# Causal masks, maxima and new turn orders in a four-layer decoder kernel

## The chip, the cores and the metric

The kernel runs on one core of a Trainium2 chip. The metric is the device time of one execution in microseconds (us). Three timed runs of the kernel before gave 1022.54, 1021.28 and 1025.13 us; the median is 1022.54 us.

## The reference

Input is `x` of 8 samples x 128 tokens x 128 features and a context of the same size, all fp32. Four layers follow one another, each an attention over the own tokens ("a"), an attention over the context ("x") and a feed-forward part ("f"), each with a residual and a normalisation. What matters here are the softmax attentions with scores of 128 queries by 128 keys per head:

- L0x: 16 heads of width 8, over the context and over the own tokens. The own tokens are masked causally.
- L1x: 16 heads of width 64, over the context, without a mask.
- L2x: 16 heads of width 8, without a mask.
- L3a: 16 heads of width 64 over the own tokens, masked causally.
- L3x: 8 heads of width 16 with exponential gates, masked causally, whose "D" term is made by the same kind of matrix products.

The others (L0a, L1a, L2a) are linear attentions; L0f, L1f, L2f are mixtures of experts of 9, 8 and 9 feed-forward blocks whose experts are all computed for all tokens.

## The kernel before, in words

The eight samples are taken in pairs (256 tokens). Two streams, a and b, run side by side: a computes pairs 0 and 2, b pairs 1 and 3. Every engine (PE = TensorE, DVE = VectorE, ACT = ScalarE, POOL = GpSimd, SP = the engine that issues DMAs) has one program per stream, written as a generator: each `yield` ends a step. `TURN_ORDER` (L144) is a table of text, one entry per engine, such as "a1 b1 a2 b1": so many steps of a, then so many of b. `take_turns` (L402) follows it, so the order of every engine's instructions is fixed when the kernel is built. Each engine then works strictly in that order, and waits on semaphores where an operand isn't there. Stream a is ahead of b by somewhat less than three stages, so that a softmax attention of one stream mostly lies beside a feed-forward part of the other. Each stream has four banks of PSUM in a ring; a bank is opened again when DVE or ACT has read it.

An attention step for one sample goes like this. `scores8` (L481, heads of width 8) or `scores64` (L771, heads of width 64) makes the scores, queries on the partitions, four heads in each of four banks. DVE takes each row's maximum (`maxima` L1179, `block_maxima` L1187) into `m_wide`, a tile whose columns 32i to 32i+3 hold the four heads of bank i. `turn_maxima` (L473) turns that tile over on PE (L479), and DVE copies the result to `mT` (L1202). Then the scores are made again with the keys on the partitions (`scores8_t` L503, `scores_t` of L1x L793 and of L3a L978), and into the same banks `less_maximum` (L491) adds a matrix product that subtracts the maximum: a column of the constant `pick` (minus one in row j), spread over 128 columns, as weights of 32 rows, and 32 rows of `mT` as the moving operand. ACT takes the exponential of each bank (L1743).

A causal mask is one more product into the same bank: the weights are `ident_bf` (128x128, bf16), and the moving operand is the 128x128 mask in bf16, repeated for the four heads (512 columns). L486, L510, L776, L984 and L1045 are these products. The products of the scores are fp32; each fp32 product is issued as two instructions, each with its own weight load, while a bf16 product is one. So 16 calls of `less_maximum` show as 32 matmuls:

```
def less_maximum(u, i, b, j, last):
    return mm(b[:, j * T:j * T + T], const("pick")[rows32(i), j:j + 1].to_broadcast([32, P]), s.mT[rows32(i), u],
              start=False, stop=last)
```

Products whose weights lie in 32 rows (`rows32`) or 64 rows (`rows64`) use a quarter or a half of the array's rows, and four or two of them can run at once. In L1x's `scores_t` four fp32 scores of 64 rows alternate, head by head, with four `less_maximum` of 32 rows.

At the start, SP loads weights in a fixed order; DVE waits for the constants (`con`), casts three of them to bf16 (L1671) and then begins its turns; ACT waits for the constants too (L2018) before its first table load. `use` (L1680) loads an ACT table when the function that is asked for is not in the table loaded last.

Of the kernel before, what the change touches and what calls it, by code (L numbers as in the profile page):

```python
# [24 lines left out]
ALU = mybir.AluOpType  # L25
# [23 lines left out]
for _n, _w in [("ident", 128), ("neg_causal", 128), ("neg_causal_t", 128), ("causal_t", 128), ("block8", 128),  # L49
               ("ones", 128), ("spread", 128), ("tiny16", 128), ("feats", 64), ("head8in32", 4), ("head16in64", 4),  # L50
               ("pick", 8), ("cos", 8), ("sin", 8), ("eps", 5)]:
    CONST[_n] = (_at, _w)
    _at += _w
# [3 lines left out]
def shape_constants():  # L57
# [9 lines left out]
    put("neg_causal", np.where(p[None, :] > p[:, None], NEG, 0).astype(np.float32))  # L67
    put("neg_causal_t", np.where(p[:, None] > p[None, :], NEG, 0).astype(np.float32))
# [7 lines left out]
    put("head16in64", (p[:, None] % 64 // 16 == np.arange(4)).astype(np.float32))  # L76
    put("pick", -(p[:, None] % 32 == np.arange(8)).astype(np.float32))
# [55 lines left out]
def group_words(g):  # L133
# [23 lines left out]
    "dve":  # L157
# [10 lines left out]
    "act":  # L168
# [8 lines left out]
    "pool":  # L177
        "a1 b1 a1 b2 a3 b1 a1 b1 a1 b1 a3 b1 a1 b2 a1 b2 a1 b1 a4 b1 a2 b4 a1 b2 a2 b2 a1 b1 a3 b1 a1 b2 a1 b2 a1 "
# [2241 lines left out]
```

## Time and profile before

| | |
|---|---|
| timed runs, median (lowest to highest) | 1022.54 us (1021.28 to 1025.13) |
| span of the profiled execution, first to last instruction | 1020.0 us |
| PE matmul busy | 904.2 us, 89% |
| DVE busy | 539.7 us, 53% |
| ACT busy | 450.7 us, 44% |
| POOL busy | 50.8 us, 5% |
| mean share of the full TensorE clock that was granted | 0.952 |
| DMA, mean over the span | 35 GB/s |

The profiled execution has no time of its own besides its span; the span is 2.5 us below the median of the runs, which is what lies around the first and the last instruction. "Busy" of PE is the time in which at least one matmul was in the array, from the modelled start of each to its end. The chain of work that ended last is followed back for only about 1% of the span (the last feed-forward part), so it says nothing of the layers before.

### The profile page before, as it was taken

Reading aid. Unit: us, or ns where it says so; the run is one execution under the profiler, and the core shown is the slowest. Engines: PE = TensorE matmul, PEld = TensorE weight load, DVE = VectorE, ACT = ScalarE, POOL = GpSimd, SP = SyncE. Lnnn points to the kernel's source line nnn. Section 1 sums busy time; section 2 is a strip of 40 time slices with the busy share of each in tenths; the row PEclk is TensorE's granted clock in tenths of the full one; section 3 lists DMA queues with packets and bytes.
Section 4 is the critical chain, followed back from the end, with each engine's and each line's share of the span. In section 5 each row is a group of like instructions: output and inputs, shape, how many; then the busy total and the mean of one; then the engine's idle time right before and its main releaser. Section 6 shows DMA issues by size and latency. Waiting matters only on the chain. (4 is left out here: it accounts for less than half of the span.)

```text
span 1020.0 us, 22561 instructions
## 1 busy us (share of the span) xinstructions
PE 904.2 (89%) x9368; PEld 700.2 (69%) x9368; DVE 539.7 (53%) x1569; ACT 450.7 (44%) x923; POOL 50.8 (5%) x71
## 2 busy tenths in 40 slices
PE   7689899999989998997987979989998989899772
PEld 5257768778778785666556757867887868686441
DVE  5733565653265575347636853655325547454345
ACT  2044343453454673574255233244465446433442
POOL 2300000010010000001000000001001000000000
PEclk8799989999999998999999999999999999999965
DMA  9100000401000301103000000040000030000000
GB/s 344 40 2 3 1 1 1 166 2 37 2 19 1 141 3 40 43 12 139 2 12 1 2 1 2 2 166 33 6 1 19 1 140 1 2 1 2 2 1 21
DMA packets 6838, 36.12 MB, mean 35 GB/s; under 512 B 721, under 2 KB 4305, under 8 KB 5458
## 3 DMA queue, kind: packets, MB, share of 16 engines
q1 hardware_dynamic: 6738, 34.68, 9.1%
q8 instruction: 76, 1.25, 0.5%
q14 instruction: 24, 0.20, 0.1%
HBM read 34.15 MB, written 0.52 MB: 34 GB/s over the span
## 5 line engine op out<-in xcount | busy, mean ns | idle before, releaser
L673 PE MATMUL bank<-xT,weights_F 128*128 128x256 f32 x832 | 202.9, 386 | 3.1 <-ACT p L1818 2.6
L673 PEld LDWEIGHTS bank<-xT,weights_F 128*128 128x128 f32 x832 | 152.0, 193 | 26.8 <-issue 4.2
L681 PEld LDWEIGHTS bank<-weights_F,p 128*128 128x128 f32 x1088 | 133.4, 191 | 18.8 <-DVE p L1363 7.2
L681 PE MATMUL bank<-weights_F,p 128*128 128x128 f32 x1088 | 141.3, 278 | 3.7 <-DVE p L1363 3.0
L1743 ACT ACTIVATE p<-bank 128x512 f32<-128x512 f32 x160 | 84.5, 601 | 121.0 <-PE bank L492 120.9
L1683 ACT ACT_TABLE_LOAD x76 | 97.5, 1283 | 12.9 <-DMA weights_con<-in_con 5.9
L1347 DVE SCALAR_TENSOR_TENSOR res<-bank,comb,res 128x128 f32<-128x128 f32 x184 | 55.7, 345 | 74.1 <-PE bank L681 71.6
L1184 DVE TENSOR_REDUCE m_wide<-bank 128x4 f32<-128x512 f32 x96 | 60.3, 684 | 43.4 <-PE bank L780 33.5
L1818 ACT ACTIVATE p<-bank 128x512 f32<-128x512 f32 x72 | 42.5, 597 | 91.6 <-PE bank L673 91.2
L1363 DVE TENSOR_TENSOR p<-p,bank 128x512 f32<-128x512 f32 x72 | 49.3, 685 | 47.5 <-PE bank L673 27.3
L1894 ACT ACTIVATE p<-bank 128x512 f32<-128x512 f32 x64 | 36.6, 598 | 51.3 <-PE bank L673 51.2
L492 PEld LDWEIGHTS bank<-mT,weights_con 32*128 32x128 f32 x1280 | 46.4, 194 | 17.4 <-issue 13.5
L492 PE MATMUL bank<-mT,weights_con 32*128 32x128 f32 x1280 | 55.1, 296 | 0.0
L1715 ACT ACTIVATE lnv<-mv,weights_con 128x2 f32<-128x2 f32 x56 | 16.6, 296 | 74.7 <-DVE mv L1139 72.7
L1192 DVE TENSOR_REDUCE mx<-bank 128x4 f32<-128x512 f32 x64 | 40.2, 682 | 16.5 <-PE bank L488 16.4
L2037 POOL TENSOR_TENSOR xb<-x_tok,biases 128x256 f32<-128x256 f32 x24 | 19.3, 806 | 575.1 <-DVE x_tok L1147 561.5
L525 PE MATMUL bank<-p,vz 128*32 128x128 f32 x1280 | 42.7, 280 | 4.5 <-ACT p L1743 4.4
L525 PEld LDWEIGHTS bank<-p,vz 128*32 128x32 f32 x1280 | 35.2, 112 | 11.0 <-issue 8.4
L525 PE MATMUL bank<-p,weights_con 128*32 128x128 f32 x1280 | 41.7, 275 | 0.0
L1207 DVE TENSOR_TENSOR attnT<-bank,res 128x128 f32<-128x128 f32 x32 | 9.3, 289 | 55.7 <-ACT res L1748 55.7
L525 PEld LDWEIGHTS bank<-p,weights_con 128*32 128x32 f32 x1280 | 35.9, 111 | 1.0
L1147 DVE TENSOR_SCALAR x_tok<-res,mv,rstd 128x128 f32<-128x128 f32 x88 | 26.4, 343 | 18.1 <-ACT rstd L1716 17.6
(319 smaller groups left out, 1356.0 us busy)
## 6 DMA issues: line engine op xcount, KB each, us to landing
weights_F<-in_L1f SPq DMA_DIRECT2D x2, 4096.0 KB, 13.8
weights_F<-in_L0f SPq DMA_DIRECT2D x2, 3456.0 KB, 13.4
weights_F<-in_L2f SPq DMA_DIRECT2D x2, 3456.0 KB, 12.1
weights_Y<-in_L1x_kv SPq DMA_DIRECT2D x2, 1024.0 KB, 10.6
weights_Z<-in_L1x SPq DMA_DIRECT2D x2, 1024.0 KB, 12.9
weights_Y<-in_L2a SPq DMA_DIRECT2D x2, 898.0 KB, 4.4
weights_Z<-in_L2x SPq DMA_DIRECT2D x2, 449.0 KB, 3.2
weights_L3m<-in_L3m SPq DMA_DIRECT2D x2, 288.0 KB, 6.1
```

The lines of the kernel that those rows point to most:

```text
L492: return mm(b[:, j * T:j * T + T], const("pick")[rows32(i), j:j + 1].to_broadcast([32, P]), s.mT[rows32(i), u], start=False, stop=last)
L525: m = mm(b[rows32(g_), cols], w, probs(g_, i), start=n == 0 and i == 0 and not (part and floor is not None), stop=n == len(blocks) - 1 and ...
L673: m = mm(b[:, k * NT:(k + 1) * NT], W[weight][:, f:f + P], s.xT[:], start=True, stop=True)
L681: m = mm(b[:, tk(u)], h[:, tk(u)], w, start=k == 0, stop=k == len(chunks) - 1)
L1184: o.count(dve.tensor_reduce(s.m_wide[:, u, 32 * i:32 * i + 4], heads(b[:], 4), X, ALU.max), free(st, "s", u, 0, i))
L1192: o.count(dve.tensor_reduce(s.mx[:, u, blk, 4 * i:4 * i + 4], heads(b[:], 4), X, ALU.max), free(st, "s", u, blk, i))
L1347: dve.scalar_tensor_tensor(r, y, s.comb[:, u, e:e + 1], r if i else s.x_tok[:, u], ALU.mult, ALU.add))
L1363: o.count(dve.tensor_tensor(s.p[:, 2 + e % 3], s.p[:, e % 2], bank(st, "up", e)[:], ALU.mult), free(st, "up", e))
L1683: act.preload_act_table_set(functions)
L1743: o.count(act.activation(s.p[:, first + i], b[:], ACT.Exp, scale=scale), free(st, "t", u, blk, i))
L1818: o.count(act.activation(s.p[:, e % 2], b[:], ACT.Silu), free(st, "gate", e))
L1894: o.count(act.activation(s.p[:, 2 * (e % 3) + half], b[:], ACT.Gelu_apprx_tanh), free("L1f", f"up{half}", e))
```

## The change

It does these things together:

- A mask is no longer a product with the 128x128 identity. `add_mask` makes it of four products per bank, each with 32 rows: weights are 32 rows of a constant that is 224 wide, cut at a different place for each k, and the moving operand is a 32x32 identity repeated for the four heads (128 columns). The banks alternate innermost, so that four products in a row use the four different groups of 32 rows.
- DVE splits each maximum into three parts (`three_parts`, two subtractions): the upper halves of fp32 words read as bf16, then the remainder, twice. They fill 12 of the 32 columns of each bank in `m_wide`. `turn_maxima` is now a bf16 product of these upper halves with `ident_bf`, `mT` is a bf16 tile, and `less_maximum` uses `pick3_bf`, which sums the three parts. PE waits for `maxima` in every stage.
- In L1x's `scores_t` all sixteen score products come first, then all of `less_maxima`.
- POOL casts the (now five) bf16 constants, in its first L0a step; DVE and ACT no longer wait for the constants at their start; ACT begins with a table load. The constants grow from 1125 to 1353 columns.
- Some waits move to a later place of their step or behind a `yield` (PE in L1a and L1x, DVE in L2x, POOL's `rest`), and ACT asks for its table once more in L3x.
- All five turn orders are new. The entries are as long as before in steps, with shorter runs: 424 runs instead of 374 for PE, 370 instead of 264 for ACT, 42 instead of 6 for SP.

```
-    put("neg_causal", np.where(p[None, :] > p[:, None], NEG, 0).astype(np.float32))
-    put("neg_causal_t", np.where(p[:, None] > p[None, :], NEG, 0).astype(np.float32))
+    away = np.arange(-96, 128)[None, :] - p[:, None] % 32
+    put("mask_s", np.where(away < 0, NEG, 0).astype(np.float32))
+    put("mask_t", np.where(away > 0, NEG, 0).astype(np.float32))
...
+    put("pick3", -((p[:, None] % 4 == np.arange(4)) & (p[:, None] % 32 < 12)).astype(np.float32))
+    put("ident32", (p[:, None] % 32 == np.arange(32)).astype(np.float32))
...
-            self.mT = own("mT", NS, T)
+            self.mT = sb(f"mT_{g}", [P, NS, T], BF16)
...
+    def upper(ap):
+        return ap.bitcast(BF16).rearrange("p (n k) -> p n k", k=2)[:, :, 1]
...
                 def turn_maxima(st, u):
                     b = opened("dve", st, "mT", u)
-                    if st == "L0x":
-                        pe.wait_ge(*told("maxima"))
-                    else:
-                        pe.wait_ge(*freed(st, "s", u, 0, 3))
-                    filled(tr(b[:, 0:T], s.m_wide[:, u], IDENT), st, "mT", u)
+                    pe.wait_ge(*told("maxima"))
+                    filled(mm(b[:, 0:T], upper(s.m_wide[:, u]), ident_bf[:], start=True, stop=True), st, "mT", u)
+
+                def add_mask(banks, mask, first=False):
+                    for k in range(4):
+                        for i, b in enumerate(banks):
+                            mm(heads(b[:], 4)[:, :, 32 * k:32 * k + 32], mask[rows32(i), 96 - 32 * k:224 - 32 * k],
+                               among(ident32_bf[rows32(i)], 4), start=first and k == 0, stop=False)
...
-                        for b in banks:
-                            mm(heads(b[:], 4), ident_bf[:], among(mask, 4), start=True, stop=False)
+                        add_mask(banks, mask, first=True)
...
-                    return mm(b[:, j * T:j * T + T], const("pick")[rows32(i), j:j + 1].to_broadcast([32, P]), s.mT[rows32(i), u],
+                    return mm(b[:, j * T:j * T + T], pick3_bf[rows32(i), j:j + 1].to_broadcast([32, P]), s.mT[rows32(i), u],
...
-                                mm(b[:, j * T:j * T + T], s.k64[rows64(r), c, tk(u)], s.q64[rows64(r), c, tk(u)], start=True, stop=False)
-                            if j == 0:
-                                pe.wait_ge(*freed("L1x", "mT", u))
-                            for n, b in enumerate(banks):
-                                m = less_maximum(u, n, b, j, True)
-                                if j == 3:
-                                    filled(m, "L1x", "t", u, 0, n)
+                                mm(b[:, j * T:j * T + T], s.k64[rows64(r), c, tk(u)], s.q64[rows64(r), c, tk(u)], start=j == 0, stop=False)
+                        less_maxima("L1x", u, banks)
...
+                def three_parts(u):
+                    wide = heads(s.m_wide[:, u], 4)
+                    top = heads(upper(s.m_wide[:, u]), 4)
+                    link(dve.tensor_tensor(wide[:, :, 4:8], wide[:, :, 0:4], top[:, :, 0:4], ALU.subtract))
+                    o.count(dve.tensor_tensor(wide[:, :, 8:12], wide[:, :, 4:8], top[:, :, 4:8], ALU.subtract), sem("maxima"))
...
+                    dve.wait_ge(*freed(st, "s", u, 0, 3))
+                    three_parts(u)
...
-            dve.wait_ge(*weights("con"))
-            for dst, src in ((ident_bf, IDENT), (neg_causal_bf, const("neg_causal")), (neg_causal_t_bf, const("neg_causal_t"))):
-                dve.tensor_copy(dst[:], src).then_inc(S("masks"), 1)
...
-            act.wait_ge(*weights("con"))
+            exp_ln()
...
+                    if pair == 0:
+                        pool.wait_ge(*weights("con"))
+                        for dst, src in ((ident_bf, "ident"), (pick3_bf, "pick3"), (ident32_bf, "ident32"), (mask_s_bf, "mask_s"), (mask_t_bf, "mask_t")):
+                            pool.tensor_copy(dst[:], const(src)).then_inc(S("masks"), 1)
```

## Rows read from the trace of the kernel before

**Rows 1.** Busy time by stretch of the span, all engines, five stretches.
```profile
core 0: us, PE busy (x) PEld busy (x) DVE busy (x) ACT busy (x) POOL busy (x), PEclk, DMA share, GB/s
0.00:100.00 100.00, 80.33 (x943) 50.85 (x944) 48.33 (x131) 29.60 (x68) 15.29 (x25) 0.88 0.28 99
100.00:390.00 290.00, 272.28 (x2549) 227.95 (x2549) 160.62 (x463) 143.82 (x258) 12.97 (x15) 0.98 0.10 36
390.00:550.00 160.00, 137.72 (x1734) 96.21 (x1730) 83.16 (x247) 77.56 (x181) 5.10 (x10) 0.97 0.09 34
550.00:915.00 365.00, 341.20 (x3340) 279.29 (x3340) 200.13 (x574) 159.46 (x304) 14.61 (x16) 0.99 0.07 26
915.00:1020.00 105.00, 72.62 (x810) 45.95 (x808) 47.44 (x155) 40.27 (x113) 2.80 (x5) 0.79 0.02 6
```
**Rows 2.** Groups of PE's instructions by line and shape: busy us, mean ns | idle before.
```profile
L492 PE MATMUL bank<-mT,weights_con 32*128 32x128 f32 x1280 | 55.1, 296 | 0.0
L798 PE MATMUL bank<-wide 64*128 64x128 f32 x256 | 22.9, 297 | 0.1
...
L507 PE MATMUL bank<-wide,qk 32*128 32x512 f32 x128 | 18.9, 646 | 3.7 <-ACT p L1743 3.1 <-DVE mT L1202 0.6
...
L780 PE MATMUL bank<-qk,wide 64*128 64x128 f32 x256 | 16.4, 278 | 0.0
...
L510 PE MATMUL bank<-neg_causal_t_bf,ident_bf 128*128 128x512 bf16 x32 | 8.3, 382 | 0.0
...
L1045 PE MATMUL bank<-neg_causal_t_bf,ident_bf 128*128 128x512 bf16 x16 | 6.1, 473 | 0.0
```
**Rows 3.** Timeline of PE, a masked L0x block: start us, us, group.
```profile
52.57 1.07 PE L507 MATMUL bank<-wide,qk 32*128 32x512 f32 x8
53.58 1.04 PE L510 MATMUL bank<-neg_causal_t_bf,ident_bf 128*128 128x512 bf16 x4
54.55 1.17 PE L492 MATMUL bank<-mT,weights_con 32*128 32x128 f32 x32
55.68 0.30 PE L479 MATMUL bank<-weights_con,m_wide 128*128 128x128 f32 x1
```
**Rows 4.** Busy time by stretch, of the instructions that read or write `ident_bf`.
```profile
0.00:100.00 100.00, 10.31 (x32) 2.79 (x32) 0.28 (x1) 0.88 0.28 99
390.00:550.00 160.00, 14.81 (x56) 4.20 (x56) 0.00 (x0) 0.97 0.09 34
915.00:1020.00 105.00, 10.95 (x36) 2.77 (x36) 0.00 (x0) 0.79 0.02 6
```
**Rows 5.** The same, of the instructions of L492.
```profile
0.00:100.00 100.00, 10.87 (x256) 10.23 (x256) 0.88 0.28 99
390.00:550.00 160.00, 11.69 (x320) 10.83 (x320) 0.97 0.09 34
915.00:1020.00 105.00, 4.69 (x128) 3.93 (x128) 0.79 0.02 6
```
**Rows 6.** Groups of PE's weight loads (PEld), by line and shape.
```profile
L492 PEld LDWEIGHTS bank<-mT,weights_con 32*128 32x128 f32 x1280 | 46.4, 194 | 17.4 <-issue 13.5
L525 PEld LDWEIGHTS bank<-p,weights_con 128*32 128x32 f32 x1280 | 35.9, 111 | 1.0
...
L510 PEld LDWEIGHTS bank<-neg_causal_t_bf,ident_bf 128*128 128x128 bf16 x32 | 2.5, 97 | 8.3 <-issue 6.4
```
**Rows 7.** Timeline of PE, one call of L1x's `scores_t`.
```profile
183.28 0.71 PE L798 MATMUL bank<-wide 64*128 64x128 f32 x8
183.93 0.50 PE L492 MATMUL bank<-mT,weights_con 32*128 32x128 f32 x8
...
187.59 0.44 PE L441 MATMUL bank<-weights_con,x_tok 128*128 128x128 f32 x2
```
**Rows 8.** Groups of DVE by line and shape: the combined maximum of L0x.
```profile
L1197 DVE TENSOR_TENSOR m_wide<-mx 128x16 f32<-128x16 f32 x8 | 1.4, 180 | 0.8
```
**Rows 9.** Groups of ACT: the table loads.
```profile
L1683 ACT ACT_TABLE_LOAD x76 | 97.5, 1283 | 12.9 <-DMA weights_con<-in_con 5.9 <-PE bank L525 5.5 <-PE bank L908 0.2
```
**Rows 10.** Waits of PE by line: us in total, times, longest us.
```profile
PE bank L726 <- DVE wide L1404: 6.1, 2, 5.0
```

More of the change, by code:

```diff
@@ L48 @@
 _at = 0
-for _n, _w in [("ident", 128), ("neg_causal", 128), ("neg_causal_t", 128), ("causal_t", 128), ("block8", 128),
+for _n, _w in [("ident", 128), ("mask_s", 224), ("mask_t", 224), ("causal_t", 128), ("block8", 128),
                ("ones", 128), ("spread", 128), ("tiny16", 128), ("feats", 64), ("head8in32", 4), ("head16in64", 4),
-               ("pick", 8), ("cos", 8), ("sin", 8), ("eps", 5)]:
+               ("pick", 8), ("pick3", 4), ("ident32", 32), ("cos", 8), ("sin", 8), ("eps", 5)]:
     CONST[_n] = (_at, _w)
@@ L145 @@
     "pe":
[11 rows of a table removed]
-    "dve":
[10 rows of a table removed]
-    "act":
[8 rows of a table removed]
[13 rows of a table added]
+    "dve":
[12 rows of a table added]
+    "act":
[11 rows of a table added]
     "pool":
-        "a1 b1 a1 b2 a3 b1 a1 b1 a1 b1 a3 b1 a1 b2 a1 b2 a1 b1 a4 b1 a2 b4 a1 b2 a2 b2 a1 b1 a3 b1 a1 b2 a1 b2 a1 "
-        "b2 a2 b2 a1 b1 ",
+        "b1 a2 b1 a4 b1 a1 b2 a2 b1 a1 b1 a1 b2 a1 b1 a2 b2 a3 b1 a1 b1 a1 b1 a1 b5 a2 b2 a4 b3 a2 b2 a1 b1 a1 b1 "
+        "a1 b2 a1 b1 ",
     "sp":
-        "a3 b6 a18 b12 a23 b26 ",
+        "a1 b3 a1 b1 a4 b1 a5 b1 a1 b1 a1 b1 a1 b1 a1 b1 a1 b1 a4 b2 a1 b4 a1 b2 a1 b4 a2 b2 a5 b6 a4 b2 a4 b2 a2 "
+        "b1 a2 b3 a1 b3 a1 b2 ",
 }
@@ L220, in _build @@
     ident_bf = sb("ident_bf", [P, P], BF16)
-    neg_causal_bf = sb("neg_causal_bf", [P, P], BF16)
-    neg_causal_t_bf = sb("neg_causal_t_bf", [P, P], BF16)
+    pick3_bf = sb("pick3_bf", [P, 4], BF16)
+    ident32_bf = sb("ident32_bf", [P, 32], BF16)
+    mask_s_bf = sb("mask_s_bf", [P, 224], BF16)
+    mask_t_bf = sb("mask_t_bf", [P, 224], BF16)
     ones_row = const("ones")[0:1, 0:128]
@@ L508, in scores8_t @@
                     if mask is not None:
-                        for b in banks:
-                            mm(heads(b[:], 4), ident_bf[:], among(mask, 4), start=False, stop=False)
+                        add_mask(banks, mask)
                     less_maxima(st, u, banks, blk)
@@ L622, in L0x @@
                     pe.wait_ge(*freed("L0x", "qk"))
-                    pe.wait_ge(S("masks"), 3)
+                    pe.wait_ge(S("masks"), 5)
                     pe.wait_ge(*told("L0x_ctx_keys"))
@@ L627, in L0x @@
                     pe.wait_ge(*told("L0x_own_keys"))
-                    scores8("L0x", 0, s.bd_k, neg_causal_bf[:], 1)
+                    scores8("L0x", 0, s.bd_k, mask_s_bf, 1)
                     yield
@@ L635, in L0x @@
                     pe.wait_ge(*told("L0x_own_keys"))
-                    scores8("L0x", 1, s.bd_k, neg_causal_bf[:], 1)
+                    scores8("L0x", 1, s.bd_k, mask_s_bf, 1)
                     yield
@@ L642, in L0x @@
                     yield
-                    scores8_t("L0x", 0, s.kT, neg_causal_t_bf[:], 1)
+                    scores8_t("L0x", 0, s.kT, mask_t_bf, 1)
                     yield
@@ L651, in L0x @@
                     yield
-                    scores8_t("L0x", 1, s.kT, neg_causal_t_bf[:], 1)
+                    scores8_t("L0x", 1, s.kT, mask_t_bf, 1)
                     yield
@@ L755, in L1a @@
                     yield
-                    pe.wait_ge(*ready("L1x_kv"))
                     for c in range(0, 8, 2):
                         yield
+                        if c == 0:
+                            pe.wait_ge(*ready("L1x_kv"))
                         by_feature("L1x", f"k{c}", "act", *((W["L1x_kv"][:, (c + k) * P:(c + k + 1) * P], s.ctxT[:]) for k in range(2)))
@@ L774, in scores64 @@
                     if mask is not None:
-                        for b in banks:
-                            mm(heads(b[:], 4), ident_bf[:], among(mask, 4), start=True, stop=False)
+                        add_mask(banks, mask, first=True)
                     for j in range(4):
@@ L785, in L1x @@
                 def L1x():
-                    pe.wait_ge(*freed("L1a", "xT"))
-                    pe.wait_ge(*ready("L1x"))
                     for c in range(0, 8, 2):
                         yield
+                        if c == 0:
+                            pe.wait_ge(*freed("L1a", "xT"))
+                            pe.wait_ge(*ready("L1x"))
                         by_feature("L1x", f"q{c}", "act", *((W["L1x_q"][:, (c + k) * P:(c + k + 1) * P], s.xT[:]) for k in range(2)))
@@ L982, in scores_t @@
                             mm(heads(b[:], 4), lat(r, u), s.q64[rows64(r), c:c + 4, tk(u)], start=True, stop=False)
-                        for b in banks:
-                            mm(heads(b[:], 4), ident_bf[:], among(neg_causal_t_bf[:], 4), start=False, stop=False)
+                        add_mask(banks, mask_t_bf)
                         less_maxima("L3a", u, banks)
@@ L995, in L3a @@
                             pe.wait_ge(*freed("L3a", "q", a, k))
-                    scores64("L3a", 0, lambda r, c: lat(r, 0), neg_causal_bf[:])
+                    scores64("L3a", 0, lambda r, c: lat(r, 0), mask_s_bf)
                     yield
@@ L999, in L3a @@
                     yield
-                    scores64("L3a", 1, lambda r, c: lat(r, 1), neg_causal_bf[:])
+                    scores64("L3a", 1, lambda r, c: lat(r, 1), mask_s_bf)
                     yield
@@ L1043, in units @@
                         banks = [opened("act", "L3x", "D", i) for i in both]
-                        for b in banks:
-                            mm(heads(b[:], 4), ident_bf[:], among(neg_causal_t_bf[:], 4), start=True, stop=False)
+                        add_mask(banks, mask_t_bf, first=True)
                         for i, b in zip(both, banks):
@@ L1196, in block_maxima @@
                             dve.wait_ge(free(st, "s", u, k, 3), ring.freed((pair, st, "s", u, k, 3))[1])
-                        o.count(dve.tensor_tensor(heads(s.m_wide[:, u], 4)[:, :, 0:4], heads(s.mx[:, u, 0], 4),
-                                                  heads(s.mx[:, u, 1], 4), ALU.max), sem("maxima"))
+                        link(dve.tensor_tensor(heads(s.m_wide[:, u], 4)[:, :, 0:4], heads(s.mx[:, u, 0], 4),
+                                               heads(s.mx[:, u, 1], 4), ALU.max))
+                        three_parts(u)
                 def pick_maxima(st, u):
@@ L1215, in softmax @@
                     if queries is not None:
+                        dve.wait_ge(*freed(st, "q"))
                         spread_heads(s.bd_q, queries, sem("queries"))
@@ L1236, in L0a @@
                     yield
+                    if turn == 0:
+                        dve.wait_ge(*weights("con"))
                     for u in range(NS):
@@ L1545, in L2x @@
                 def L2x():
-                    dve.wait_ge(*freed("L2x", "q"))
                     yield
@@ L1775, in L0a @@
                     act.wait_ge(*told("L0a_den"))
+                    if turn == 0:
+                        act.wait_ge(*weights("con"))
                     inverse(s.res[:, 0], s.res[:, 0])
@@ L2016, in program @@
                         yield from stage()
-            act.wait_ge(*weights("con"))
+            exp_ln()
             take_turns("act", program)
@@ L2039, in rest @@
                 def rest(then=None):
-                    pool.wait_ge(*told("x_new", NS))
+                    done = told("x_new", NS)
                     if then:
+                        pool.wait_ge(*done)
                         then()
```

65 rows, old and new, of the table TURN_ORDER are left out of this document.

## The prediction

> **What bounds the kernel now.** The chain that ended last reaches back only over the end of the kernel, so I read busy time by stretch first [rows 1], and looked at what each engine leaves idle. PE is busy 904 of 1020 us, DVE and ACT about half. In 100 to 390 and 550 to 915 us PE is idle for 41.5 of 655 us (6%): one stream's attention lies beside the other's feed-forward part, and PE sets the time. In the other three stretches it is idle for 74.3 of 365 us (20%). I call these the crowded stretches: both streams are in attention stages, or there is only one left, and PE waits for DVE and ACT. The granted clock says the same: 0.98 and 0.99 of full speed (2.4 GHz) in the two dense stretches, 0.88, 0.97 and 0.79 in the crowded ones. Then I read the groups of PE by shape, for what the changed products cost [rows 2], the timeline of one block of them [rows 3], and the busy time by stretch of these products alone, for where they lie [rows 4, 5].
>
> **What a small bf16 product costs.** In the timeline the four masks begin at 53.58 and the next group at 54.55 [rows 3]: 0.97 us. Four of 512 columns lasted 1.04 from first start to last end, and one takes 0.382 [rows 2]; so the starts are (1.04 - 0.38)/3 = 0.22 apart, 0.055 per 128 columns. The remaining 0.97 - 4 x 0.22 = 0.1 is the changeover from 128-row weights to 32-row ones. For fp32, L507's eight instructions are two rounds of four 32-row products that run at once. They last 1.07, one of them 0.646 [rows 2, 3]: the rounds are 0.43 apart at 512 columns, 0.107 at 128. I take 0.11 for an fp32 round of 128 columns and 0.06 for a bf16 one. The trace has no bf16 round of four 32-row products. The bounds are 0.055 (the array alone, as above) and 0.11 (no faster than an fp32 round, the nearest shape). I take the lower part because the weight load does not seem to hold it up. An fp32 load takes 111 ns for 32 columns and 194 for 128 [rows 6], so 0.86 ns a column on a fixed 83; the bf16 load of 128 columns takes 97, so only some 14 ns belong to its columns.
>
> A rule of the Trainium skill speaks against that. "TensorE: Matmul & The Clock Gate", section "LDWEIGHTS (loading the stationary operand)", states that a load takes its columns divided by 1.2 and that 32 rows cost as much as 128. An estimate from that page is thus 107 ns per load of 128 columns, in which case a bf16 round would take as long as an fp32 one. The fp32 rows agree with its slope (0.86 against 0.83 ns a column), the bf16 row does not.
>
> **Maxima (L492).** 16 calls are 32 fp32 instructions, eight rounds of four; they become 16 bf16 instructions, four rounds. Saved: 8 x 0.11 - 4 x 0.06 = 0.64 us a block. There are 1280 instructions [rows 2], 40 blocks; eight belong to L1x, so 32 x 0.64 = 20.5 us.
>
> **Masks.** Lines 486, 510, 776 and 984 have 32 instructions each (L510 stands for them [rows 2]), 32 blocks of four. A block of 0.97 becomes four rounds of 0.06, 0.24. In 24 blocks the neighbour is a 32-row product too, so the changeover goes: 0.73 each. In the eight of L3a's `scores64` 64-row products follow and 0.1 stays: 0.63 each. Together 22.6. L3x has eight pairs (L1045, 16 instructions [rows 2]): two 512-column products and a changeover, 0.54, become four rounds of two, 0.24: 2.4. At the lower clock L486 costs more; I add 1. Masks: 26 us.
>
> **L1x.** One call lasts from 183.28 to 187.59, 4.31 us [rows 7]: eight groups, each of another tile shape than the last. Afterwards the 32 fp32 instructions of 64 rows run as those of `scores64` do. L780 has two groups of 16.4 us for 16 blocks [rows 2], 2.05 each, with the last one's end. With four bf16 rounds that is 2.3, so 2.0 saved, eight times: 16 us.
>
> **The turned maxima** go from one fp32 instruction of 0.30 to one bf16 of perhaps 0.27: 1 us in all.
>
> PE loses 20.5 + 26 + 16 + 1 = 63.5 us of work. **Where it lies:** 22 of the 32 plain blocks of L492 are in the crowded stretches (704 of 1280 instructions [rows 5]), and 124 of 144 masks [rows 4]. So 14 + 22.5 = 36.5 us come out of the crowded stretches and 27 out of the dense ones. In the dense ones I count a tenth as lost, somewhat more than their idle share; in the crowded ones 30%, since DVE's reads of the scores and ACT's exponentials stay as they are and become late next: 2.7 + 11 = 13.7 given back. Net 49.8.
>
> **Added on DVE.** Two small subtractions per maximum, 64, like L1197's 0.18 [rows 8], about 0.2 with the wait between: 13 us of DVE's idle 480. On the path each turn of the maxima comes 0.4 later, and the other stream's DVE work behind them as well. In the new PE order 20 of the 32 turns have feed-forward steps or a projection of the other stream ahead of them, which cover it; 12 have attention steps or transposes only: 12 x 0.4 = 4.8 us.
>
> **ACT.** I followed `use` along both orders: three more table loads, of 1.28 [rows 9], 3.8 us on an engine that is idle more than half the time. Between 0 and 3.8; I take 1.
>
> **Start.** ACT's first load waits 5.9 us for the constants [rows 9] and then takes 1.28; the new kernel loads before. Between 0 and 1.3 saved, since the second stream's input lands at about that time too; I take 1. POOL's five casts cost nothing: POOL is busy 15 of the first 100 us [rows 1], and the first mask is far behind. The same holds for the constants' 228 more columns, which first matter when a transpose needs them; if they land late, this 1 us is gone. The waits that move inside a step, and SP's order, I cost at nothing: PE's largest waits are for DVE, not for a load.
>
> **Orders.** The longest wait between the start and the end is 5.0 us, in which PE stands at L726 for DVE's decay of L1a [rows 10]. Before, only a projection of b came ahead of that step; now b's transposes, gate and the first two sets of L0f products (some 5 us) are there. That is worth 5. From other such places I take 3, with bounds of 0 and 12.
>
> **Sum:** -49.8 + 4.8 + 1 - 1 - 8 = -53.0. The profiled span of 1020.0 is 2.5 below the median run, and I carry that difference over: span 967.0, time 1022.5 - 53.0 = **969.5 us**. A measurement of this kernel can tell about 0.5% (5 us) from no change.
>
> **Rivals.**
>
> *Loads pace the small products.* A bf16 round takes 0.11. Then a plain L492 block saves 0.44, a mask block 0.2 less, L3x 0.2 less a pair, L1x 0.2 less a call: 6.4 + 6.4 + 1.6 + 1.6 = 16 less, 47.5 removed, 37 kept (78%, as above), 13 less than in the sum, and the time is 982. For it: nothing in the trace shows the faster round. Against it: the bf16 load of 97 ns [rows 6]. Chance 0.20. It is what the skill's rule on loads, cited above, would give.
>
> *PE stays dense.* The new orders fit the new durations, idle time stays at its 116 us in all [rows 1], nothing is given back, and the orders gain 10: 1022.5 - 63.5 - 10 = 949. For it: every removed piece sits in a list of steps that was laid anew, and 89% of the span is PE work. Against it: the crowded stretches are already held by DVE and ACT. Chance 0.25.
>
> *The clock falls (slower).* With shorter bursts between the same waits PE is granted 1.2 instead of 2.4 GHz for longer. The crowded stretches would hold 290.7 - 36.5 = 254 us of PE work, at a mean grant of about 0.90 now [rows 1]. At 0.70 that is 254 x 0.90/0.70 = 327, 73 more: 1042. It decides from a grant of 0.74 on, where the 53 us are used up. For it: 0.79 in the last stretch. Against it: 0.97 in the middle one, with the same kind of steps. Chance 0.05.
>
> *The change doesn't reach the time.* PE's work shrinks, but the chain through DVE and ACT sets the time in the crowded stretches, and the added subtractions and table loads (13 + 4 us) use up what the dense ones gain: about 1020. Against it: the 6% of idle time in the dense stretches, from which 27 us go. Chance 0.04.
>
> **How the numbers follow.** The likeliest case, as summed, has 0.46 and its own range is 955 to 985: 30% given back could be 15 or 50% (6 us either way), the orders 0 to 12. The range of 940 to 998 takes in the loads' case and most of the dense one, and leaves out the two that end near or above 1020. Faster by over 0.5%: 0.46 + 0.20 + 0.25 = 0.91; within: 0.04; slower: 0.05.
>
> **What would show it.** In the changed profile: PE busy near 840 us; L492 with 640 instructions and some 20 us; a mask block of 16 instructions in about 0.3 us, a round of four 0.06 apart (0.11 if the loads pace); an L1x call of about 2.3 us; about 64 subtractions of 0.18 on DVE; PE idle about 126 us, most of the growth in the crowded stretches; no long wait at L1a's decay; 79 table loads. The prediction is wrong if PE's busy time falls by 60 and the span doesn't follow by at least 40, or if the granted clock in the crowded stretches is far from 0.90.

## The result, and the profile after

The changed kernel takes 1009.51 us (median of 4 runs, 1007.26 to 1014.45), the kernel before 1021.91 (4 runs). The ratio is 0.9879, with a 95% interval of 0.9848 to 0.9911: faster by 1.2%, where 5% was forecast. 1009.5 lies above the range of 940 to 998. The profiled execution is the slowest of the four, 1014.45 us with a span of 1012.4.

The page of the changed kernel first: busy time, and the granted clock in 40 slices.

```profile
span 1012.4 us, 22200 instructions
## 1 busy us (share of the span) xinstructions
PE 863.6 (85%) x9160; PEld 684.8 (68%) x9160; DVE 549.6 (54%) x1630; ACT 449.3 (44%) x923; POOL 51.4 (5%) x76
...
PEclk9678979999999999998979699999999999999975
```

PE is busy 40.6 us less than before, not 63.5 less, and idle 148.8 us (1012.4 - 863.6) instead of 115.8 (1020.0 - 904.2). The five stretches of [rows 1], at the same borders:

```profile
0.00:100.00 100.00, 70.16 (x849) 46.76 (x850) 47.30 (x119) 26.53 (x63) 16.36 (x30) 0.80 0.28 100
100.00:390.00 290.00, 265.20 (x2437) 221.24 (x2436) 151.63 (x456) 143.79 (x251) 11.43 (x13) 0.96 0.09 33
390.00:550.00 160.00, 130.29 (x1660) 95.33 (x1658) 89.47 (x259) 75.96 (x176) 5.36 (x9) 0.93 0.11 40
550.00:915.00 365.00, 329.63 (x3319) 272.24 (x3320) 206.28 (x622) 160.87 (x320) 15.59 (x19) 0.96 0.07 26
915.00:1012.40 97.40, 68.33 (x902) 49.20 (x900) 54.91 (x178) 42.16 (x116) 2.68 (x5) 0.81 0.02 7
```

Read the granted clock, the third column from the right: it is lower than before in the first four stretches, and even the two dense ones, at 0.96, have more idle time (60.2 us where [rows 1] have 41.5).

What answers to [rows 2, 6], PE's and PEld's groups by line and shape. L512 is the maxima (was L492), L499 the masks (was L510 and its like), L818 L1x's transposed scores (was L798), L493 the turned maxima, L692 a feed-forward group that the change does not touch.

```profile
L692 PE MATMUL bank<-xT,weights_F 128*128 128x256 f32 x832 | 212.2, 400 | 4.7 <-ACT p L1842 2.5 <-DVE res L1373 2.2
L512 PE MATMUL bank<-mT,pick_bf 32*128 32x128 bf16 x640 | 18.1, 226 | 0.0
L818 PE MATMUL bank<-wide 64*128 64x128 f32 x256 | 16.4, 278 | 0.4 <-ACT p L1765 0.3
L499 PE MATMUL bank<-ident_bf,mask_t_bf 32*128 32x128 bf16 x320 | 11.2, 234 | 0.0
L493 PE MATMUL bank<-ident_bf,m_wide 128*128 128x128 bf16 x32 | 7.2, 225 | 13.6 <-DVE m_wide L1197 13.5
L499 PE MATMUL bank<-ident_bf,mask_s_bf 32*128 32x128 bf16 x256 | 6.8, 222 | 4.5 <-DVE mx L1214 1.9 <-ACT wide L1985 1.7 <-DVE mT L1225 1.0
```
```profile
L512 PEld LDWEIGHTS bank<-mT,pick_bf 32*128 32x128 bf16 x640 | 13.9, 99 | 10.1 <-issue 8.9
```

And the timeline of PE, a masked L0x block and one call of L1x's scores (answers to [rows 3, 7]; start us, us, group).

```profile
58.15 0.41 PE L499 MATMUL bank<-ident_bf,mask_t_bf 32*128 32x128 bf16 x16
58.38 0.41 PE L512 MATMUL bank<-mT,pick_bf 32*128 32x128 bf16 x16
60.07 0.22 PE L493 MATMUL bank<-ident_bf,m_wide 128*128 128x128 bf16 x1 [1.29 <-DVE m_wide L1197]
...
191.08 2.06 PE L818 MATMUL bank<-wide 64*128 64x128 f32 x32
193.07 0.40 PE L512 MATMUL bank<-mT,pick_bf 32*128 32x128 bf16 x16
```

The products cost what was forecast. Four bf16 rounds last 0.23 us from start to start (58.15 to 58.38), 0.058 a round against 0.06. The masks' two groups are 18.0 us, the maxima's 18.1 instead of 55.1. An L1x call lasts 191.08 to 193.47, 2.39 us against 2.3. But L692, with the same 832 products, went from 386 to 400 ns each, 9.3 us more in all. That is the clock: where PE's waits are filled (e13 below, the same orders at a clock of 0.965) the same products take 386 ns again.

Last, PE's waits (us in total, times, longest), where [rows 10] had 6.1 for the decay, and DVE's two added subtractions.

```profile
PE bank L458 <- DVE x_tok L1160: 23.7, 15, 6.9
PE bank L475 <- DVE attnT L1230: 13.7, 10, 3.6
PE bank L493 <- DVE m_wide L1197: 13.5, 14, 2.5
PE bank L475 <- DVE attnT L1543: 7.3, 3, 4.2
```
```profile
L1196 DVE TENSOR_TENSOR m_wide<-m_wide 128x16 f32<-128x16 f32 x32 | 7.0, 220 | 1.1
L1197 DVE TENSOR_TENSOR m_wide<-m_wide 128x16 f32<-128x16 f32 x32 | 5.6, 175 | 1.1
```

L458 is the turned x and L475 the projection. PE waits there 23.0 us in all for the attention's result (13.7, 7.3 and 2.0 at a third line). In the trace of before the same waits are 15.5 us for x and 4.7 for the attention's result (3.9, 0.5 and 0.3). What is missing from the forecast is in these rows and in the clock; the experiments had to say which part of the change puts it there.

### The profile page after: what moved, and what is told of

It is laid out like the page before. It is cut to its first block and busy times, and to the rows that moved or that the text cites. A ratio compares the mean times of both kernels' runs of the same rounds, so it can differ in the third digit from the quotient of the medians.

```text
span 1012.4 us, 22200 instructions
## 1 busy us (share of the span) xinstructions
PE 863.6 (85%) x9160; PEld 684.8 (68%) x9160; DVE 549.6 (54%) x1630; ACT 449.3 (44%) x923; POOL 51.4 (5%) x76
## 5 line engine op out<-in xcount | busy, mean ns | idle before, releaser
L692 PE MATMUL bank<-xT,weights_F 128*128 128x256 f32 x832 | 212.2, 400 | 4.7 <-ACT p L1842 2.5
L692 PEld LDWEIGHTS bank<-xT,weights_F 128*128 128x128 f32 x832 | 158.6, 200 | 35.3 <-issue 8.3
L700 PEld LDWEIGHTS bank<-weights_F,p 128*128 128x128 f32 x1088 | 136.0, 194 | 10.2 <-DVE p L1389 2.9
L1737 ACT ACTIVATE lnv<-mv,weights_con 128x2 f32<-128x2 f32 x56 | 16.6, 296 | 82.5 <-DVE mv L1152 74.1
L1214 DVE TENSOR_REDUCE mx<-bank 128x4 f32<-128x512 f32 x64 | 40.6, 683 | 13.9 <-PE bank L508 13.7
L458 PE MATMUL bank<-weights_con,x_tok 128*128 128x128 f32 x88 | 19.7, 309 | 23.7 <-DVE x_tok L1160 23.7
L1230 DVE TENSOR_TENSOR attnT<-bank,res 128x128 f32<-128x128 f32 x32 | 9.3, 290 | 51.5 <-ACT res L1770 51.3
L508 PE MATMUL bank<-wide,qk 32*128 32x512 f32 x192 | 30.2, 704 | 8.2 <-DVE mT L1225 4.3
## 6 DMA issues: line engine op xcount, KB each, us to landing
weights_F<-in_L1f SPq DMA_DIRECT2D x2, 4096.0 KB, 12.7
weights_F<-in_L2f SPq DMA_DIRECT2D x2, 3456.0 KB, 11.8
```

The lines of the kernel that those rows point to most:

```text
L508: filled(mm(heads(b[:], 4), s.qT[rows32(i), tk(u)], keys[rows32(i), u], start=mask is None, stop=True), st, "s", u, blk, i)
L692: m = mm(b[:, k * NT:(k + 1) * NT], W[weight][:, f:f + P], s.xT[:], start=True, stop=True)
L700: m = mm(b[:, tk(u)], h[:, tk(u)], w, start=k == 0, stop=k == len(chunks) - 1)
L1214: o.count(dve.tensor_reduce(s.mx[:, u, blk, 4 * i:4 * i + 4], heads(b[:], 4), X, ALU.max), free(st, "s", u, blk, i))
```

## The experiments

Medians are of 4 runs (5 and 6 in two cases); each ratio is to the kernel before on the same chip, with its 95% interval. The moved waits and the new start are in all of them. "Old" and "new orders" are `TURN_ORDER` of before and after.

**Products and orders apart.** The new operations with the old orders on all five engines:

```diff
 TURN_ORDER = {
     "pe":
-        "a1 b1 a2 b2 a3 b1 a2 b2 a2 b3 ...
+        "a1 b1 a2 b1 a2 b1 a2 b3 a1 b1 ...
```


> The changed kernel with the five turn orders of before. Theory A (the new orders cost what the smaller products gave): 970 to 985 us, granted clock back to about 0.95, PE's waits for attnT and x_tok as before. Theory B (the products' time was never worth much: DVE and ACT set the time in the crowded stretches, and a less busy PE is granted a lower clock): 1000 to 1012 us, clock 0.92 to 0.94, whichever the orders.

988.2 us, 0.967 (0.9625 to 0.9716): between the two theories, near the first. The page of this run, and PE's waits in it (x, the turned maxima, L1a's decay):

```profile
span 982.8 us, 22199 instructions
PE 852.9 (87%) x9160; PEld 677.6 (69%) x9160; DVE 550.4 (56%) x1630; ACT 450.4 (46%) x922; POOL 51.6 (5%) x76
```
```profile
PE bank L450 <- DVE x_tok L1152: 18.7, 16, 7.6
PE bank L485 <- DVE m_wide L1189: 11.8, 13, 2.0
PE bank L737 <- DVE wide L1422: 11.5, 4, 5.0
```

And the reverse, the new orders with the old masks, fp32 maxima and L1x:

```diff
-  mm(b[:, 0:T], upper(s.m_wide[:, u]), ident_bf[:], start=True, stop=True)
+  tr(b[:, 0:T], s.m_wide[:, u], IDENT)
...
-  for k in range(4): ... mask[rows32(i), 96 - 32 * k:224 - 32 * k]
+  for b in banks: mm(heads(b[:], 4), ident_bf[:], among(mask[:], 4), ...)
```


> New orders, moved waits and the new start, but masks, maxima and the order inside L1x's second scores as before. Theory A: the orders alone cost 25 to 45 us, 1045 to 1065 us. Theory B: the orders are about neutral, 1015 to 1028 us.

1061.84 us, 1.037 (1.033 to 1.041), as in theory A. The orders alone cost 37 us, and with the new products 21 (1009.5 against 988.2). The products alone give 3.3%, 34 us, and under the new orders about 50 (1.037 against 0.9879). So the change is two effects of opposite sign that don't simply add, and the loss came out of the part that had been costed at -8.

**The products one by one, old orders.** Masks alone; maxima and L1x alone; masks and L1x; masks and maxima. In short, what each puts back as it was before:

```diff
 e3  - three_parts(u), pick3_bf, less_maxima in L1x      (masks stay)
 e4  - 32-row mask tiles                                  (maxima, L1x stay)
 e5  - three_parts(u), pick3_bf                           (masks, L1x stay)
 e6  - less_maxima after L1x's scores                     (masks, maxima stay)
```


> Old orders, new masks alone; maxima and L1x as before. PE loses some 23 us of work. Theory A: 15 to 20 us faster than before (1002 to 1007). Theory B: 3 to 8 us faster (1014 to 1019), with a lower granted clock.

991.94 us, 0.969 (0.9644 to 0.9736): 10 us better than either theory. PE's line of its page:

```profile
PE 872.6 (88%) x9800; PEld 698.6 (71%) x9800; DVE 540.1 (55%) x1566; ACT 449.6 (45%) x922; POOL 52.4 (5%) x76
```

> Old orders, old masks; maxima in three bf16 parts and L1x's scores in one tile shape at a time. PE loses some 44 us of work, DVE gains 64 small subtractions. Theory A: 28 to 36 us faster (986 to 994). Theory B: 5 to 15 us faster (1007 to 1017), since each turn of the maxima comes 0.4 us later.

1005.56 us, 0.983 (0.9794 to 0.9866): near theory B.

> Old orders; new masks and L1x's scores in one tile shape at a time, but the maxima whole in fp32 (no subtractions on DVE). The masks alone gave 33 us, all parts together 37. Theory C (what the maxima's parts save on PE is taken back by PE's waits for the two subtractions): the L1x order adds its 1.3 us a call, some 10 us, 978 to 984 us, better than all parts together. Theory D (after the masks PE's work is not worth more, whichever part it is): 988 to 993 us.

988.08 us, 0.9634 (0.9597 to 0.9671): theory D's number.

> Old orders; new masks and maxima in three parts, L1x alternating as before. Theory C: 990 to 998 us, no better than the masks alone, with PE waiting some 11 us for the maxima where it waited 4. Theory D: 987 to 991 us.

984.56 us, 0.9614 (0.9593 to 0.9635): better than both theories, though PE waits 12.4 us for the maxima, as theory C had it.

3.1% and 1.7% make 4.8%, and together they make 3.3 (e1): the gains don't add. On top of the masks, L1x alone gave 4 us and the maxima alone 7, and both together 4 (988.2), which by the intervals can't be told from either. The masks take 31.6 us from PE's busy time (904.2 to 872.6) and 31.7 from the time (3.1% of 1022.5). With the maxima and L1x on top, PE's busy time falls by another 20 (852.9 in e1), and the time hardly moves. The profiles say where it stops: PE's idle time is 117.4 us with the masks alone (990.0 - 872.6) and 129.9 in e1; its waits for DVE's `m_wide` go from 4.4 us to 11.8, and the mean granted clock from 0.956 to 0.936 (0.950 to 0.961 over the runs of e3, 0.926 to 0.936 over those of e1).

**Moving PE's steps.** Two tries to cover waits by PE's order alone. Under the old orders, L1a's decay (11.5 us of waits in e1) behind 3, 1, 1 and 1 steps of the other stream:

```diff
-0:L1a decay, 1:L0x turn_x, 0:L1a qT, 1:L0f gates, 0:L1a kT, 1:L0f dn0
+1:L0x turn_x, 1:L0f gates, 1:L0f dn0, 0:L1a decay, 0:L1a qT, 0:L1a kT
```


> All new parts, old orders but for PE's four steps that turn L1a's decay over: three, one, one and one steps of the other stream go ahead of them. PE waits 11.5 us for DVE there in the run with the old orders. If a wait is worth its own length where the other stream has work to give: 977 to 983 us, and the low clock behind the first of them is gone. If it only moves on to the next step: 985 to 990 us.

989.56 us, 0.9657 (0.9628 to 0.9687): nothing. The decay's waits are gone, PE now waits 4.0 us at one place for ACT's `p`, and its waits for x go from 18.7 to 23.4 us: the wait moved on. Under the new orders, ten projections that have no step of the other stream ahead of them, each one or two such steps later:

```diff
-0:L0a proj, 1:L0a o, 0:L0a before, 0:L0a turn_x, 1:rows2
+1:L0a o, 1:rows2, 0:L0a proj, 0:L0a before, 0:L0a turn_x
```


> The changed kernel, with its new orders but for ten projections in PE's order: one or two steps of the other stream go ahead of each, since eight of 24 now follow their stream's own step at once (one before). PE waits 23 us for attnT there. If uncovered projections are what the new orders cost: 990 to 998 us. If the cost lies all over the orders: 1003 to 1010 us.

1029.23 us, 1.005 (1.0032 to 1.0067), 20 us slower than the changed kernel and outside both theories. The wait at the projection falls from 13.7 to 6.1 us, and others grow: those for x from 23.7 to 39.4 us, and PE waits 7.7 us for the normalised x inside L2a, behind two of the moved projections, where the changed kernel waits 0.6. A projection heads a chain through DVE and ACT back to PE, the next x among it; later on PE, it makes all of that later.

**Which stretch.** The traces of e1 and of the changed kernel, cut at the same three places (the turned x of pair 0's L0f and pair 1's L0x; of 0's L3x and 1's L2f; of 2's L1a and 3's L0x). First e1, then the changed kernel; the columns are those of [rows 1].

```profile
0.00:118.00 118.00, 92.90 (x1166) 68.16 (x1166) 62.19 (x169) 39.34 (x85) 17.04 (x31) 0.91 0.24 85
118.00:450.00 332.00, 304.72 (x2976) 249.71 (x2976) 190.08 (x570) 178.21 (x327) 13.51 (x18) 0.96 0.10 37
450.00:604.00 154.00, 129.96 (x1782) 96.01 (x1783) 98.41 (x278) 61.55 (x154) 6.87 (x9) 0.94 0.06 24
604.00:983.00 379.00, 325.29 (x3238) 263.71 (x3236) 199.70 (x618) 171.27 (x356) 14.18 (x18) 0.91 0.07 27
```
```profile
0.00:133.00 133.00, 99.28 (x1159) 71.82 (x1160) 62.66 (x170) 44.76 (x90) 17.09 (x31) 0.83 0.21 76
133.00:483.00 350.00, 313.46 (x2982) 255.59 (x2984) 188.98 (x563) 174.52 (x325) 13.38 (x18) 0.96 0.09 34
483.00:651.00 168.00, 136.86 (x1797) 101.49 (x1794) 98.23 (x284) 65.41 (x160) 6.86 (x9) 0.89 0.07 24
651.00:1013.00 362.00, 314.01 (x3231) 255.86 (x3229) 199.71 (x614) 164.62 (x351) 14.09 (x18) 0.94 0.08 28
```

The counts in brackets are nearly equal, so each pair of rows is the same work. The new orders lose 15, 18 and 14 us in the first three stretches, of which 25 are idle time and 22 busy time, and win 17 in the last. (The two traces differ by 29.6 us and the medians by 21.3: e1's trace is of its fastest run, the changed kernel's of its slowest.) That suggested a kernel that takes the old orders first and the new ones from the third cut on:

```diff
-"pe": the order of before, all 724 steps
+"pe": the order of before for a's first 244 and b's first 208 steps, the new order for the rest
 (DVE cut at 294 and 254, ACT at 247 and 219; POOL and SP as before)
```


> The changed kernel's products and subtractions with PE's, DVE's and ACT's steps in the order of before up to the turned x of pair 2's L1a on stream a and of pair 3's L0x on stream b (PE steps 244 and 208), and in the new order from there; POOL and SP in the order of before. In the traces the old orders come to that place at 602 us and 606 us, the new ones at 655 and 646; from there the old ones need 377 us to the end of the span, the new ones 357. Theory P, each order costs what its own stretch shows, wherever it stands: 606 + 357 = 963 us of span, about 966 us of time, faster than both kernels and some 22 us under the old orders all through (988.2). Theory Q, the new orders only catch up in the last third because their streams come to it closer together or further behind, and an order does not carry its time to another start: 985 to 1000 us, no better than the old orders.

973.75 us, 0.9516 (0.9488 to 0.9545), nearer to 966 than to 985 and faster than both kernels. The reverse:

```diff
+"pe": the new order for a's first 244 and b's first 208 steps, the order of before for the rest
```


> The reverse of the run before: the new order of PE's, DVE's and ACT's steps up to the same place, the order of before from there. Theory P: 655 + 377 = 1032 us of span, about 1034 us of time, 22 us over the changed kernel (1009.5). Theory Q: 1005 to 1018 us, the same as the changed kernel within the noise.

1028.19 us, 1.0041 (0.9989 to 1.0092), against the 1034 and the 1005 to 1018 expected. In its trace the four stretches last 133, 352, 165 and 377 us, like the first three of the changed kernel and the last of e1. An order's cost stays with its stretch, to within 8 us. And the load queues alone:

```diff
 e1, with
-"pool": order of before, "sp": order of before
+"pool": new order, "sp": new order
```


> The changed kernel's products with PE's, DVE's and ACT's steps in the order of before and the load queues (POOL's and SP's) in the new order. If the loads' order has no part in the 21 us that the new orders cost: 988 us plus or minus 3, as with the old orders on all five engines. If it is where they lose (weights issued later on these queues): 1000 us or more.

982.86 us, 0.9608 (0.958 to 0.9637), a little under the 985 to 991 expected: the loads have no part in the loss. Which of the other three orders, PE's, DVE's or ACT's, carries it wasn't tried.

**Waits or clock.** In the traces the new orders lose idle time and clock together (0.936 in e1's, 0.925 in the changed kernel's), and each could be the cause of the other. Over all four runs of each, though, the clock is the same: 0.926 to 0.936 in e1, 0.925 to 0.936 in the changed kernel. To settle it, the next kernels keep PE at work in its longest waits:

```diff
+def fill(b, st, what):
+    for _ in range(FILL.get((pair, st, what), 0)):
+        mm(heads(b[:], 4), ident_bf[:], among(ident_bf[:], 4), start=True, stop=True)
 def turn_x(st):
     b = opened("act", st, "xT")
+    fill(b, st, "x")
     pe.wait_ge(*told("x_new", NS))
```
First in e9:

> The run that took the old orders first and the new ones later, and in 15 of the places where its PE waits longest (five turned maxima, three decays, three turned x, two projections and two second products of L2a) 4 to 30 products of 128 rows by 512 columns in bf16, 145 in all, written to the bank that the step has just opened and overwritten by the step's own product: their result is used nowhere. They only keep PE at work while it waits. In the trace of the run without them these 15 waits last 36 us together, and 67 of the 112 us at the lower clock follow one of them within a few us. Theory K, the granted clock falls because PE rests, and the lower clock then costs time of its own: the granted clock rises from 0.943 to 0.96 or more and the time falls from 973.8 by 10 to 25 us, to 949 to 964. Theory N, what the clock costs is hidden by the waits, or the clock does not follow these waits: 970 to 985, with whatever the fillers add where they run past the end of a wait.

969.29 us, 0.9481 (0.9444 to 0.9518), at a clock of 0.964: 4.5 us, between the two theories. One group of fillers stood at the wrong projection: the wait of 4.2 us was pair 3's L2a. Then in the changed kernel:

> The changed kernel with its own orders, and in the 17 longest of PE's waits that have a bank open (44.5 us in its trace) 172 products of 128 rows by 512 columns in bf16 whose result is overwritten at once and used nowhere. Theory K, the clock carries the loss: the granted clock rises from about 0.93 to 0.955 or more and the time falls from 1009.5 by 12 us or more, to under 998. Theory W, the new orders' waits for the vector and the scalar engine carry it, and PE's slower work lies inside them: the clock rises as much, but the time falls by 6 us or less, to 1003 or more (under the old orders the same filling raised the clock from 0.943 to 0.964 and took 4.5 us).

992.92 us, 0.973 (0.971 to 0.9751), 16.6 us less, at 0.965. (What its expectation calls the old orders is e12, the mixture.) Here is one wait in the two traces, the turned x of pair 1's L0a at 32 us: the changed kernel, then this run.

```profile
31.00:37.00 6.00, 1.41 (x25) 0.61 (x19) 4.71 (x14) 0.50 (x2) 0.99 (x2) 0.77 0.16 48
37.00:52.00 15.00, 8.48 (x52) 4.31 (x51) 13.12 (x25) 0.96 (x2) 8.50 (x12) 0.64 0.05 16
52.00:84.00 32.00, 25.30 (x499) 16.09 (x502) 12.81 (x28) 12.98 (x26) 0.00 (x0) 0.79 0.01 2
```
```profile
31.00:37.00 6.00, 4.76 (x43) 2.46 (x42) 3.72 (x11) 0.48 (x3) 0.73 (x1) 0.96 0.03 6
37.00:52.00 15.00, 11.12 (x79) 5.27 (x76) 14.59 (x30) 0.99 (x3) 9.22 (x12) 1.00 0.11 33
52.00:84.00 32.00, 26.12 (x594) 17.20 (x598) 13.67 (x32) 13.56 (x28) 0.00 (x0) 0.95 0.01 3
```

PE rests for most of 31 to 37 us, and from 37 to 52 its granted clock is 0.64, a mixture of 1.2 and 2.4 GHz; with the wait filled it is 1.00. From 52 to 84 us the same 32 us hold 594 products, 8 of them fillers, instead of 499. "TensorE: Matmul & The Clock Gate" of the Trainium skill, section "HAM oscillation — how this bites in real kernels", tells of the same fall of the clock where PE waits for a DMA between bursts. These rows show it for a wait on DVE, 0.64 against 1.00.

By this run alone the clock would seem to carry the new orders' loss. Two controls say otherwise. e12 with its misplaced group moved:

```diff
-(2, "L2x", "y"): 17
+(3, "L2a", "y"): 17
```


> The run e12_busy_waits with its group of 17 products moved from the projection of pair 2's L2x, which does not wait, to that of pair 3's L2a, which waits 4.2 us at 805 us. If the group cost what 17 products in a dense place cost (17 x 0.21 = 3.6 us) and the clock after the wait at 805 us costs a further 1 to 2 us: 969.3 - 4 to 6 = 963 to 966 us. If under these orders the clock has little to give: 967 to 970.

961.1 us, 0.9382 (0.9338 to 0.9426), at 0.969: 12.7 us less than e9, under the 963 to 966 expected, and the fastest kernel of all. And e1 with its 17 longest waits filled:

```diff
 e1, with fill() as above and
+FILL = {(0, "L2f", "x"): 4, (3, "L1f", "x"): 5, ..., (0, "L1a", "decay"): 20, (1, "L1a", "decay"): 7, ...}
```


> The old orders with the new products (988.2 us), and in the 17 longest of PE's waits that have a bank open (39.4 us in that run's trace) 146 products of 128 rows by 512 columns in bf16 whose result is overwritten at once and used nowhere. If the clock costs every order alike, the time falls by 11 to 17 us, to 971 to 977, and stays 16 to 22 us under the filled new orders (992.9): the orders then differ by PE's waits. If the clock sets the orders apart, the time falls by 5 us or less, to 983 to 988.

969.97 us, 0.9472 (0.9441 to 0.9504), at 0.963: 18.2 us less than e1, a little more than the 11 to 17 expected. The filling gives every order about as much: filled, the two orders are 23 us apart (969.97 and 992.92), unfilled 21. The pages of the two filled kernels, old orders first, then new:

```profile
span 969.2 us, 22477 instructions
...
PE 870.5 (90%) x9306; PEld 677.1 (70%) x9306; DVE 550.1 (57%) x1630; ACT 449.6 (46%) x922; POOL 51.5 (5%) x76
```
```profile
span 989.1 us, 22532 instructions
...
PE 871.6 (88%) x9332; PEld 678.4 (69%) x9332; DVE 548.7 (55%) x1630; ACT 448.8 (45%) x923; POOL 51.9 (5%) x76
```

And the fillers in the two, old orders first, then PE's feed-forward group in the second (L692 of the changed kernel):

```profile
L453 PE MATMUL bank<-ident_bf 128*128 128x512 bf16 x146 | 36.1, 393 | 0.7 <-DMA weights_Z<-in_L2x 0.7
L461 PE MATMUL bank<-ident_bf 128*128 128x512 bf16 x172 | 40.1, 380 | 1.3 <-DVE biases L1294 1.2
L704 PE MATMUL bank<-xT,weights_F 128*128 128x256 f32 x832 | 202.5, 386 | 4.7 <-ACT p L1855 2.5 <-DVE res L1386 2.2
```

At the same clock (0.963 and 0.965) PE's own work, without the fillers, takes 834.4 us (870.5 - 36.1) and 831.5 (871.6 - 40.1). The spans differ by 19.9: what differs is the rest, idle time and fillers together, 134.8 against 157.6 us. The new orders are slower by PE's waits for DVE and ACT. The clock is a second cost beside them, of 13 to 18 us, that the three kernels with their longest waits filled had (e13, e14, e15). In e1 and e15 one sees it alone: the same orders and products, and PE's own work takes 852.9 us at 0.936 and 834.4 at 0.963.

## Why the prediction was wrong

The sum was -53.0; -13 came. Two steps failed: the new orders, put at -8, cost 21 us, and the clock, which the sum put at nothing, took back what the products were short of. By the prediction's own steps:

- **PE's work** (-20.5, -26, -16, -1): right. Rounds of 0.058 us, masks and maxima of 18 us each, L1x calls of 2.39. Added up over the traces, each product from the end of the one before it, the changed products take 113.9 us before, 45.3 in e1 and 46.1 in the changed kernel: 68 to 69 less, where 63.5 was forecast. The *loads pace* rival (0.11 a round) is refuted by the timeline. The round was right for another reason than the one given, that few of a bf16 load's ns belong to its columns: a load lasts longer than a round (99 against 58 ns), but 640 of them keep PEld busy for only 13.9 us, 22 ns each, so loads run beside each other. The rule of "TensorE: Matmul & The Clock Gate" of the Trainium skill, section "LDWEIGHTS (loading the stationary operand)", makes an estimated 107 ns a load of 128 columns. The trace agrees for one load (99 ns); that a round takes as long, which I had drawn from it, the trace does not show (58 ns).
- **Orders (-8): the step that failed.** They cost 21 us with the new products (e1) and 37 without them (e2). I priced them by one wait that they remove. That wait did go: PE's waits for the decay are 11.5 us in e1 and none in the changed kernel, where 3.7 us, 2.0 at the longest, stand at the step behind it. But the same lists bring other steps up to their waits. Of 24 projections, 8 now have no step of the other stream ahead of them, 1 before, and PE's waits for the attention's result go from 4.7 us to 23.0. The bounds of 0 and 12 us gained left out any loss, which nothing in the trace excluded. Counting such steps would not have given the price either: e8 covers all but one of the 24 by PE's order alone and is 20 us slower. No single place carries the loss: it is spread over the first 650 us, and why it is as large as it is stays open beyond that.
- **The clock (0 in the sum): too small, and the whole of what the products were short of.** Without the orders' step the sum was -45.0, and e1 gives 3.3% of 1022.5, which is 33.7: 11 us short. In e1's trace PE's busy time falls by 51.3 us where 63.5 was forecast, though the changed products gave their share. The other 7656 products, which the change leaves alone, take 790.3 us before and 807.5 in e1 (817.5 in the changed kernel's trace), and 790.8 and 788.3 where the waits are filled (e15, e13). So the loss is in the lower clock (0.952 before, 0.936 in e1), and by this count most of it is new. As a rival the clock stood at 0.05, with 0.74 in the crowded stretches as its point of decision. They came to 0.80, 0.93 and 0.81 (0.88, 0.97 and 0.79 before), so it didn't decide. But I had treated it as all or nothing, and it takes 13 to 18 us in the kernels that were filled. The kernel before wasn't filled.
- **DVE (+4.8) and what is given back (13.7).** The waits for `m_wide` are 11.8 us in e1 and 13.5 in the changed kernel, where the trace of before has 4.2: 7.6 and 9.3 us more instead of 4.8. 12 turns had been counted as uncovered; 14 wait in the changed kernel, 5 before. The total was not too small: with ACT's 1 and the start's -1 these terms make 18.5 us of idle time, and in e1 it grew by 14.1 (115.8 to 129.9). In the changed kernel it grew by 33, the rest with the orders.
- **ACT and start**: 79 table loads, as forecast. What the start gave wasn't tried alone.
- *PE stays dense* and *the change doesn't reach the time* are both out: idle time grew by 33 us, and the products do reach the time (e1).

By way of e1, 11 us from the products' side and 29 from the orders' (-8 against +21) make the 40 between 969.5 and 1009.5. By way of e2 the orders miss by 45 (-8 against +37), and the products then give some 50, 5 more than their -45. Either way the orders are the larger miss. The test that I had named, busy time down by 60 and a span that doesn't follow by 40, wouldn't have caught this: PE's busy time fell by 40.6 only, since the lower clock put part of the work back.

## What to carry to other kernels

An order of several in-order engines is a change of its own: run it apart from the operations that it was made for, and cut both traces at the same steps, since orders that lose in one stretch may win in the next (here: -47 and +17 us, and a mixture that beats both). A wait that an order removes says little of what it costs, and so does a count of the steps that have no work of the other stream ahead of them: taking 11.5 us of waits away in e7 gave nothing, and covering the projections in e8 cost 20 us. And when PE's work shrinks and its waits grow, look at the granted clock of the same products: keeping PE at work in its longest waits with products that nobody reads gave 13 to 18 us here.

## What the runs showed of the hardware

- Unread products in a wait were worth more than they cost. 146 of them in e15 raised the granted clock from 0.936 to 0.963 and took 18.2 us off the time, though DVE and ACT did the same work.
- Rounds of four 32-row bf16 products of 128 columns started 0.058 us apart, while each of their weight loads lasted 99 ns.
- The lower clock came with the maxima in three parts, not with less PE work as such. With the masks alone PE's busy time fell by 31.6 us, at a mean clock of 0.950 to 0.961 over the runs (0.947 to 0.953 before on the same chip). Under the old orders the 7656 products that no run changes take 787.8 to 794.9 us with whole maxima (before, e3, e5) and 805.0 to 807.5 with split ones (e4, e6, e1). There PE's waits for `m_wide` are 11.2 to 12.4 us instead of 4.2 to 4.4; that these waits are the link is likely, since filling waits raised the clock, but no run fills them alone.
